# A finer account of time behind the order of two woven streams, and a later start for eight sets of blanks

## The chip, the cores and the metric

The kernel runs on one core of one Trainium2 chip. The time is device microseconds (us) of one launch, and the median over several launches counts. The core has five instruction queues that matter here: PE (TensorE, matmuls and transposes), ACT (ScalarE), DVE (VectorE), POOL (GpSimd) and SP (it only starts DMAs). Each works through its own instructions strictly in the order in which the program was written and waits for the others on semaphores. If the instruction at the head of a queue waits, everything behind it waits too.

## The reference

The model is a chain of sixteen residual steps on x of shape (8, 256, 128) in float32. Each one is `x = x + f(layernorm(x))`:

```
x = x + mamba(ln(x));             x = x + experts(ln(x))
x = x + linear_attention(ln(x));  x = x + experts(ln(x))
x = x + windowed_attention(ln(x)); x = x + channel_mix(ln(x))
x = x + delta_rule(ln(x));        x = x + channel_mix(ln(x))
x = x + state_space(ln(x));       x = x + low_rank_linear(ln(x))
x = x + mixed_attention(ln(x));   x = x + low_rank_linear(ln(x))
x = x + causal_attention_a(ln(x)); x = x + deep_network(ln(x))
x = x + causal_attention_b(ln(x)); x = x + deep_network(ln(x))
```

The two causal attentions have sixteen heads of eight elements. The state-space step is computed as a convolution with a filter that is worked out from its matrices A, B and C.

## The kernel before

**Two streams.** The batch of eight sequences is cut into four pairs, and a pair (512 tokens) goes through a layer at a time. Stream a takes pairs 0 and 2, stream b pairs 1 and 3. Each stream has four of the eight PSUM banks and its own working memory. Both run phase one (`mamba` to the second `channel_mix`) for their first pair and then for their second. They meet in `state_space`, which needs all four pairs, and then run phase two (`low_rank_linear` to the second `deep_network`) twice each. In the trace `stream_a` and `stream_b` are the buffers that hold a stream's normalized tokens and their transpose.

**How the order is made.** A layer is written as one Python generator for each engine (`tensor`, `scalar`, `vector`, `pool`, `sync`). It yields the signals that it waits for. The class `Weave` merges the lanes (one engine's program in one stream) into one order for each engine while the program is built. It keeps an account of time: each engine has a `free` time, each issued instruction adds a cost (`Lane.matmul`, `activation`, `vector` and others, L94 to L163), and its signals carry the time at which they would be raised. `Weave.run` (L222) always advances the lane with the smallest key:

```
key = (max(ready, e.free), lane.rank == BEHIND, ready, lane.rank)
```

`ready` is the accounted time of the signal that the lane waits for. So of the lanes of one engine the one whose signal came first goes first, and the costs decide which one that is. Nothing of this account exists at run time: only the order of the instructions in each queue is left of it.

**The lane behind.** `prepare` (L1765) computes the state-space filter on DVE and POOL (`product`, `power`, `back`, `ahead`, `filter`). It has the rank `BEHIND`, so it goes last among lanes whose time is equal. When its result is stored, `filter_loads` reloads the weights of the windowed attention (`held_l1a`), whose place in memory the filter's inputs had taken; the second pair's windowed attention waits for them.

**The blanks.** `small_heads` (L2179) is both causal attentions. Its heads are padded from 8 to 32 columns, and POOL writes the padding in five memsets (`wide_q`, `wide_k` twice, `wide_v` twice). Before them it waits for `s.rstd` (L2321), the signal for which the vector engine waits before it centres the tokens (`normalize`, L360 and after: four `tensor_scalar`, one for each 128 tokens, `stream_a<-x,moments,rstd` in the trace). PE's transposes of `wide_k` need the second blank, DVE's `placed` the fifth. Both also need the projected and copied q, k and v. `small_heads` is run eight times: two layers for four pairs.

## Time and profile before

| what | value |
|---|---|
| median of 3 runs | 3211.99 us (3210.1 to 3213.61) |
| the profiled execution | 3234.81 us |
| its span, first to last instruction | 3233.5 us |
| PE busy | 2634.1 us, 81% |
| DVE busy | 2104.3 us, 65% |
| ACT busy | 1429.0 us, 44% |
| POOL busy | 578.4 us, 18% |
| mean granted TensorE clock | 0.896 |

The span is one profiled execution. It lies 22.8 us above the median of the plain runs. Busy time of PE includes matmuls that run at the lower of the two clock levels, so it shrinks when the clock rises. An instruction is named by its source line: all matmuls are L108, transposes L111, activations L121, two-input vector operations L129, `tensor_scalar` L132, `scalar_tensor_tensor` L135, reductions L138, memsets L159. A float32 matmul is two instructions in the trace.

### The profile page before, as it was taken

The numbers are of one execution on the slowest core, as the hardware profiler recorded it, in microseconds if no ns is written. First come the engines' busy times: TensorE is split into PE (matmuls) and PEld (weight loads), VectorE is DVE, ScalarE is ACT, GpSimd is POOL, SyncE is SP. The second block draws the span as 40 slices with busy tenths as digits, with TensorE's granted clock in tenths as the row PEclk, the third lists the DMA queues.
The fourth block names the chain that finished last, engine by engine and source line by source line (L and its number), as shares of the span: only waits on it lengthen the run. The fifth ranks groups of instructions, "written<-read, shape, count | busy, mean of one in ns | idle before, by whom it ended". The sixth has DMA issues, their size and how long they took to land. (4 is left out here: it accounts for less than half of the span.)

```text
span 3233.5 us, 41136 instructions
## 1 busy us (share of the span) xinstructions
PE 2634.1 (81%) x15734; PEld 1707.1 (53%) x15734; DVE 2104.3 (65%) x4051; ACT 1429.0 (44%) x2577; POOL 578.4 (18%) x482
## 2 busy tenths in 40 slices
PE   5789897884878578989788689769878989778888
PEld 1267674452675224757454458459755455444554
DVE  6977887879988998888788675451264243552331
ACT  5533336774533553333477663340134335334342
POOL 2700001218760163000122064000010100000000
PEclk8999898996986699999889899569879999789899
DMA  3000001110000000000211200008200000000000
GB/s 146 0 1 1 1 1 33 40 34 4 1 1 1 0 1 32 1 1 1 76 40 40 66 1 2 0 1 273 86 1 2 1 1 1 7 1 1 1 2 7
DMA packets 51924, 73.18 MB, mean 23 GB/s; under 512 B 5776, under 2 KB 41360, under 8 KB 51088
## 3 DMA queue, kind: packets, MB, share of 16 engines
q1 hardware_dynamic: 51728, 70.56, 7.1%
q8 instruction: 124, 2.03, 0.3%
q14 instruction: 72, 0.59, 0.1%
HBM read 52.32 MB, written 1.44 MB: 17 GB/s over the span
## 5 line engine op out<-in xcount | busy, mean ns | idle before, releaser
L108 PEld LDWEIGHTS ps<-held_ffn,hidden 128*128 128x128 f32 x2304 | 299.4, 192 | 160.6 <-issue 110.4
L121 ACT ACTIVATE grown<-ps,bias_grown 128x512 f32<-128x512 f32 x288 | 197.9, 687 | 340.1 <-PE ps L108 333.6
L108 PE MATMUL ps<-held_ffn,hidden 128*128 128x128 f32 x2304 | 308.1, 277 | 24.4 <-DVE hidden L135 23.9
L129 POOL TENSOR_TENSOR qk<-conv,held_const 128x512 f32<-128x512 f32 x64 | 93.8, 1467 | 981.0 <-DVE conv L135 981.0
L135 DVE SCALAR_TENSOR_TENSOR conv<-conv_in,held_l1a,conv 128x512 f32<-128x512 f32 x288 | 228.5, 804 | 40.4 <-ACT conv L121 33.0
L129 POOL TENSOR_TENSOR long<-long,product 128x512 f32<-128x512 f32 x136 | 202.2, 1509 | 131.2 <-ACT product L121 123.6
L135 DVE SCALAR_TENSOR_TENSOR hidden<-ps,bias_kept,grown 128x512 f32<-128x512 f32 x288 | 211.6, 745 | 4.2
L132 DVE TENSOR_SCALAR grown<-grown,bias_fallen 128x512 f32<-128x512 f32 x288 | 140.1, 486 | 95.2 <-ACT grown L121 92.8
L159 POOL MEMSET wide_q<- 128x1536 f32 x8 | 11.0, 1378 | 978.9 <-ACT rstd L121 978.9
L129 POOL TENSOR_TENSOR part<-state,c_rows 128x512 f32<-128x512 f32 x128 | 163.1, 1302 | 97.3 <-issue 57.0
L138 DVE TENSOR_REDUCE wide_q<-ps 128x4 f32<-128x512 f32 (+1 forms) x128 | 114.4, 950 | 94.8 <-PE ps L108 94.7
L108 PE MATMUL ps<-part,held_const 128*128 128x512 f32 x256 | 151.2, 679 | 8.7 <-POOL part L129 5.3
L108 PE MATMUL ps<-stream_a,held_ffn 128*128 128x512 f32 x288 | 147.8, 597 | 2.3 <-ACT stream_a L121 2.3
L108 PE MATMUL ps<-stream_b,held_ffn 128*128 128x512 f32 x288 | 148.7, 601 | 0.7 <-ACT stream_b L121 0.7
L141 DVE TENSOR_TENSOR_SCAN state<-decay,ps 128x512 f32<-128x512 f32 x128 | 146.3, 1195 | 0.0
L108 PE MATMUL ps<-yn,nT 128*128 128x192 f32 (+1 forms) x640 | 113.8, 326 | 39.3 <-DVE yn L129 21.6
L121 ACT ACTIVATE probs<-ps 128x768 f32<-128x768 f32 x128 | 96.5, 808 | 97.4 <-PE ps L108 97.2
L144 DVE COPY outT<-ps 128x256 f32<-128x256 f32 x64 | 27.0, 421 | 156.7 <-PE ps L108 156.3
L108 PEld LDWEIGHTS ps<-yn,nT 128*128 128x128 f32 x640 | 100.1, 204 | 47.1 <-issue 36.6
L108 PE MATMUL ps<-u,ring 128*128 128x128 f32 (+3 forms) x1024 | 114.5, 275 | 1.2 <-DVE u L129 1.2
L108 PEld LDWEIGHTS ps<-u,ring 128*128 128x128 f32 x1024 | 114.4, 192 | 1.6 <-DVE u L129 1.6
L108 PE MATMUL ps<-a,held_l3f 128*128 128x512 f32 x256 | 111.6, 593 | 0.1
(442 smaller groups left out, 5717.1 us busy)
## 6 DMA issues: line engine op xcount, KB each, us to landing
ring<-lags SPq DMA_DIRECT2D x64, 512.0 KB, 4.5
turned<-conv SPq DMA_DIRECT2D x256, 64.0 KB, 2.0
held_ffn<-in_ffn SPq DMA_DIRECT2D x1, 4690.0 KB, 19.0
held_l1a<-in_l1a SPq DMA_DIRECT2D x2, 2120.0 KB, 15.9
held_l3f<-in_l3f SPq DMA_DIRECT2D x1, 2824.0 KB, 12.4
held_rows<-in_rows SPq DMA_DIRECT2D x1, 1044.5 KB, 8.3
out<-x SPq DMA_DIRECT2D x4, 256.0 KB, 2.6
held_const<-in_const SPq DMA_DIRECT2D x1, 785.0 KB, 4.6
```

Of the source, the lines that this page charges most:

```text
L108: return self.sent(self.real.matmul(out, lhsT, rhs, **kw), cost, 0.15)
L121: return self.sent(self.real.activation(out, a, func, **kw), cost)
L129: return self.vector(self.real.tensor_tensor(out, a, b, op), columns(out))
L132: return self.vector(self.real.tensor_scalar(out, a, p, q, *ops), columns(out))
L135: return self.vector(self.real.scalar_tensor_tensor(out, a, p, b, first, second), columns(out))
L138: return self.vector(self.real.tensor_reduce(out, a, axis, op, **kw), columns(a))
L141: return self.sent(self.real.tensor_tensor_scan(out, a, b, first, one, two), 0.16 + columns(out) / 460)
L144: return self.vector(self.real.tensor_copy(out, a), columns(out))
L159: return self.vector(self.real.memset(out, value), columns(out) // 2)
```

## The change

Four things are changed in the account, and one wait in the kernel. None of the arithmetic changes.

- PE's cost no longer is one number for each matmul. `Engine.blocks` is a grid of 4 by 4 array blocks with a time for each, so matmuls with a `tile_position` on different blocks may overlap and those on the same one queue. `Clock` keeps a level, fast or slow, by how much accounted matmul work fell into each past stretch, and doubles the cost of what starts in a slow one. Matmuls of four columns or fewer don't count as work.
- A vector operation without a PSUM operand, and every POOL operation that goes through `vector`, also waits for `Weave.shared`, one time that both engines share: they exclude each other in the account.
- Costs and tails of ACT, DVE and POOL instructions get other constants, the wait instruction costs nothing, and reciprocals, reductions and scans have formulas of their own.
- The first element of the key becomes `max(ready, e.free + 0.5)`, so a lane behind is taken only if no other lane of the same key time up to half a microsecond after `free` is ready.
- In `small_heads` POOL's blanks wait for `s.centred` at NT (all four centrings done) in place of `s.rstd`.

The diff:

```diff
@@ -59,11 +59,44 @@
     ACT.Sigmoid: 2}
 
 
+class Clock:
+
+
+    STRETCH, LITTLE, FULL = 3.41, 0.53, 0.9
+
+    def __init__(self):
+        self.fast = True
+        self.end = self.STRETCH
+        self.busy = 0.0
+        self.done = 0.0
+
+    def at(self, t):
+        while t >= self.end:
+            share = self.busy / self.STRETCH
+            self.fast = share >= self.LITTLE if self.fast else share >= self.FULL
+            self.end += self.STRETCH
+            self.busy = 0.0
+        return 1 if self.fast else 2
+
+    def worked(self, begin, end):
+        begin = max(begin, self.done)
+        if end <= begin:
+            return
+        self.done = end
+        if end > self.end:
+            self.busy += max(0.0, self.end - begin)
+            begin = max(begin, self.end)
+            self.at(self.end)
+        self.busy += end - begin
+
+
 class Engine:
 
     def __init__(self, name, real):
         self.name, self.real = name, real
         self.free = 0.0
+        self.blocks = np.zeros((4, 4))
+        self.clock = Clock()
         self.known = {}
         self.table = None
         self.spare = []
@@ -91,72 +124,87 @@
     def wait_ge(self, signal, n):
         return signal, n
 
-    def sent(self, ins, cost, latency=0.06):
+    def sent(self, ins, cost, tail):
         e = self.engine
         e.free += cost
-        return Sent(self, ins, e.free + latency)
+        return Sent(self, ins, e.free + tail)
+
+    def array(self, ins, cost, narrow=False, rows=slice(0, 4), cols=slice(0, 4)):
+        e = self.engine
+        begin = max(e.free, e.blocks[rows, cols].max())
+        slow = e.clock.at(begin)
+        end = begin + cost * slow
+        if not narrow:
+            e.clock.worked(begin, end)
+        e.blocks[rows, cols] = end
+        whole = e.blocks[rows, cols].size == e.blocks.size
+        e.free = end if whole else begin + 0.016
+        return Sent(self, ins, end + 0.15 + 0.05 * slow)
 
     def matmul(self, out, lhsT, rhs, **kw):
         n = columns(rhs)
-        slow = lhsT.dtype == F32
-        m = lhsT.shape[-1]
-        cost = max(n, 64) * (1.7 if slow else 0.43) / 1000
-        if "tile_position" in kw:
-            cost = cost / 3 + 0.015
-        else:
-            cost = max(cost, 0.225 if slow else 0.06)
-        return self.sent(self.real.matmul(out, lhsT, rhs, **kw), cost, 0.15)
+        ins = self.real.matmul(out, lhsT, rhs, **kw)
+        cost = max(n / 600, 0.223) if lhsT.dtype == F32 else max(n / 2400, 0.06)
+        if "tile_position" not in kw:
+            return self.array(ins, cost, n <= 4)
+        r, c = kw["tile_position"]
+        return self.array(ins, cost, n <= 4, slice(r // 32, (r + lhsT.shape[0] + 31) // 32),
+                          slice(c // 32, (c + lhsT.shape[-1] + 31) // 32))
 
     def transpose(self, out, a, ident):
-        return self.sent(self.real.transpose(out, a, ident), 0.112, 0.15)
+        return self.array(self.real.transpose(out, a, ident), 0.109)
 
     def activation(self, out, a, func, **kw):
-        cost = 0.19 + columns(out) / 960
         table = FUNCTION_SETS.get(func)
         if table is not None and table != self.engine.table:
             self.engine.table = table
-            cost += 1.3
+            self.engine.free += 1.3
             if table is EXP_AND_LN:
                 self.real.preload_act_table_set(EXP_AND_LN)
-        return self.sent(self.real.activation(out, a, func, **kw), cost)
-
-    def vector(self, ins, n):
-        if self.engine.name == "POOL":
-            return self.sent(ins, 0.12 + n / 400, 0.1)
-        return self.sent(ins, 0.16 + n / 960)
+        return self.sent(self.real.activation(out, a, func, **kw), 0.13 + columns(out) / 1150, 0.14)
+
+    def vector(self, ins, n, *of):
+
+        e, w = self.engine, self.weave
+        pool = e.name == "POOL"
+        cost = 0.1 + n / 460 if pool else 0.065 + n / 960
+        if pool or not any(a.space.name == "PSUM" for a in of):
+            e.free = max(e.free, w.shared)
+            w.shared = e.free + cost
+        return self.sent(ins, cost, 0.15 if pool else 0.13)
 
     def tensor_tensor(self, out, a, b, op):
-        return self.vector(self.real.tensor_tensor(out, a, b, op), columns(out))
+        return self.vector(self.real.tensor_tensor(out, a, b, op), columns(out), out, a, b)
 
     def tensor_scalar(self, out, a, p, q, *ops):
-        return self.vector(self.real.tensor_scalar(out, a, p, q, *ops), columns(out))
+        return self.vector(self.real.tensor_scalar(out, a, p, q, *ops), columns(out) // 2 + 40, out, a)
 
     def scalar_tensor_tensor(self, out, a, p, b, first, second):
-        return self.vector(self.real.scalar_tensor_tensor(out, a, p, b, first, second), columns(out))
+        return self.vector(self.real.scalar_tensor_tensor(out, a, p, b, first, second), columns(out) + 60, out, a, b)
 
     def tensor_reduce(self, out, a, axis, op, **kw):
-        return self.vector(self.real.tensor_reduce(out, a, axis, op, **kw), columns(a))
+        return self.sent(self.real.tensor_reduce(out, a, axis, op, **kw), 0.065 + columns(a) / 960, 0.13)
 
     def tensor_tensor_scan(self, out, a, b, first, one, two):
-        return self.sent(self.real.tensor_tensor_scan(out, a, b, first, one, two), 0.16 + columns(out) / 460)
+        return self.sent(self.real.tensor_tensor_scan(out, a, b, first, one, two), 0.04 + columns(out) / 480, 0.13)
 
     def tensor_copy(self, out, a):
-        return self.vector(self.real.tensor_copy(out, a), columns(out))
+        return self.vector(self.real.tensor_copy(out, a), columns(out), out, a)
 
     def reciprocal(self, out, a):
-        return self.vector(self.real.reciprocal(out, a), columns(out))
+        return self.sent(self.real.reciprocal(out, a), 0.065 + columns(out) / 150, 0.13)
 
     def max(self, out, a):
-        return self.vector(self.real.max(out, a), columns(a))
+        return self.sent(self.real.max(out, a), 0.065 + columns(a) / 960, 0.13)
 
     def bn_stats(self, out, a):
-        return self.vector(self.real.bn_stats(out, a), columns(a))
+        return self.sent(self.real.bn_stats(out, a), 0.065 + columns(a) / 960, 0.13)
 
     def bn_aggr(self, out, a):
-        return self.vector(self.real.bn_aggr(out, a), 24)
+        return self.sent(self.real.bn_aggr(out, a), 0.08, 0.12)
 
     def memset(self, out, value):
-        return self.vector(self.real.memset(out, value), columns(out) // 2)
+        return self.vector(self.real.memset(out, value), columns(out) // 2, out)
 
     def dma_start(self, out, a):
         self.engine.free += 0.1
@@ -177,6 +225,7 @@
         self.engines = {name: Engine(name, real) for name, real in (
             ("PE", nc.tensor), ("ACT", nc.scalar), ("DVE", nc.vector), ("POOL", nc.gpsimd), ("SP", nc.sync))}
         self.made = 0
+        self.shared = 0.0
 
     def raised(self, lane, signal, ins, by, at):
         engine = lane.engine
@@ -213,7 +262,6 @@
             if e.known.get(signal.sem.num, 0) < signal.base + n:
                 e.known[signal.sem.num] = signal.base + n
                 e.real.wait_ge(signal.sem, signal.base + n)
-                e.free += 0.02
         try:
             lane.asked = next(lane.program)
         except StopIteration:
@@ -229,7 +277,7 @@
                     ready = 0.0 if lane.asked is None else lane.asked[0].when(lane.asked[1])
                     if ready is None:
                         continue
-                    key = (max(ready, e.free), lane.rank == BEHIND, ready, lane.rank)
+                    key = (max(ready, e.free + 0.5), lane.rank == BEHIND, ready, lane.rank)
                     if best is None or key < best[0]:
                         best = key, lane
             if best is None:
@@ -2318,7 +2366,7 @@
 
     def pool(po):
         yield from n_.pool(po)
-        yield po.wait_ge(s.rstd, 1)
+        yield po.wait_ge(s.centred, NT)
         po.memset(b.wide_q[:, :, :, D:], 0.0).then_inc(s.blank)
         po.memset(c.wide_k[:, :, :, D:D + 1], 1.0).then_inc(s.blank)
         po.memset(c.wide_k[:, :, :, D + 1:], 0.0).then_inc(s.blank)
```

## Rows read from the trace of the kernel before

**Rows 1.** The page, part 1: busy time, share of the span, instructions.
```profile
PE 2634.1 (81%) x15734; PEld 1707.1 (53%) x15734; DVE 2104.3 (65%) x4051; ACT 1429.0 (44%) x2577; POOL 578.4 (18%) x482
```

**Rows 2.** Busy time by stretch: window, engines' busy us, PEclk, DMA share, GB/s.
```profile
730.00:1090.00 360.00, 252.62 (x1395) 190.52 (x1396) 331.83 (x513) 155.39 (x255) 183.91 (x148) 0.76 0.01 1
...
1850.00:2185.00 335.00, 268.17 (x1444) 203.35 (x1445) 199.53 (x407) 150.87 (x244) 89.78 (x68) 0.79 0.00 1
...
2330.00:2760.00 430.00, 370.90 (x2731) 219.52 (x2732) 173.64 (x397) 176.04 (x284) 20.88 (x24) 0.93 0.00 1
2760.00:3180.00 420.00, 344.47 (x2675) 209.67 (x2673) 163.57 (x359) 152.96 (x255) 21.00 (x24) 0.91 0.01 2
```

**Rows 3.** Timeline of DVE at the end: stream a behind stream b's network.
```profile
3174.08 0.26 DVE L147 RECIPROCAL inverse<-ps 128x16 f32<-128x16 f32 x1 [13.91 <-PE ps L111]
```

**Rows 4.** Last projection before the state-space step, by stream.
```profile
L108 PE MATMUL ps<-held_l2a,stream_a x16: 379/380/634, 2136.3 to 2151.3; 128*128 128x256 f32 x16
...
L108 PE MATMUL ps<-held_l2a,stream_b x16: 379/559/634, 2167.3 to 2181.3; 128*128 128x256 f32 x16
```

**Rows 5.** The chain that ended last, in order of time: start us, us, what.
```profile
2377.83 3.00 DVE stream_b L132 x3
...
2583.08 4.45 DVE stream_a L132 x3
...
2986.75 3.13 DVE stream_b L132 x4
```

**Rows 6.** Timeline of DVE, 2370 to 2400 us: start us, us, what, instructions.
```profile
2370.07 1.12 DVE L132 TENSOR_SCALAR stream_b<-x,moments,rstd 128x128 f32<-128x128 f32 x4 [1.27 <-ACT rstd L121]
...
2390.20 1.74 DVE L129 TENSOR_TENSOR qkv<-qkv,held_rows 128x1536 f32<-128x1536 f32 x1
...
2397.47 1.76 DVE L129 TENSOR_TENSOR qkv<-qkv,held_rows 128x1536 f32<-128x1536 f32 x1 [2.59 <-ACT qkv L121]
```

**Rows 7.** Timeline of POOL, same stretch: the first blank and the last.
```profile
2377.85 1.38 POOL L159 MEMSET wide_q<- 128x1536 f32 x1 [391.28 <-ACT rstd L121]
...
2390.07 1.58 POOL L159 MEMSET wide_v<- 128x64 f32 x2
```

**Rows 8.** Groups of instructions by form: busy us, mean ns, idle before.
```profile
L132 DVE TENSOR_SCALAR grown<-grown,bias_fallen 128x512 f32<-128x512 f32 x288 | 140.1, 486 | 95.2 <-ACT grown L121 92.8
...
L121 ACT ACTIVATE probs<-ps 128x768 f32<-128x768 f32 x128 | 96.5, 808 | 97.4 <-PE ps L108 97.2
...
L129 DVE TENSOR_TENSOR product<-power 128x1024 f32<-128x1024 f32 x24 | 53.9, 2246 | 0.3
```

**Rows 9.** Timeline of PE in windowed attention, 600 to 612 us.
```profile
604.52 0.76 PE L108 MATMUL ps<-probs,v 128*64 128x192 f32 x8
...
605.12 0.71 PE L108 MATMUL ps<-probs,ones 128*64 128x192 f32 x8
...
605.76 1.16 PE L108 MATMUL ps<-held_const,square 128*128 128x128 f32 x8
```

**Rows 10.** Timeline of PE in small heads, 2879 to 2891 us.
```profile
2881.18 0.94 PE L108 MATMUL ps<-kT,qT 32*128 32x128 f32 x16 [1.13 <-DVE wide_q L138]
...
2882.05 0.61 PE L108 MATMUL ps<-after,ident 128*128 128x256 bf16 x4
...
2882.59 0.94 PE L108 MATMUL ps<-qT,kT 32*128 32x256 f32 x16
```

**Rows 11.** Mixed attention's casts of each stream: first and last start.
```profile
L144 DVE CAST x<-stream_a x2: 421/424/426, 2338.5 to 2786.9; 128x512 f16<-128x512 f32 x2
...
L144 DVE CAST x<-stream_b x2: 428/428/428, 2333.7 to 2751.3; 128x512 f16<-128x512 f32 x2
```

**Rows 12.** Reload and first use of held_l1a in the second pass.
```profile
L108 PEld LDWEIGHTS ps<-stream_a,held_l1a x30: 186/190/338, 1559.4 to 1682.3; 128*128 128x128 f32 x30
...
L164 SPq DMA_DIRECT2D held_l1a<-in_l1a x1: 344/344/344, 1277.2 to 1277.2; - x1
```

**Rows 13.** Busy time in the stretch from the second mamba to that use.
```profile
1087.00:1620.00 533.00, 439.11 (x2024) 261.72 (x2022) 448.58 (x896) 232.62 (x392) 94.40 (x76) 0.93 0.05 17
```

## The prediction

> **What bounds the kernel now.** The page's busy times come first [rows 1]. PE works 81% of the span, DVE 65%, and no engine is full, so the time is PE's work plus the stretches in which PE waits. The account that the change rewrites can touch only the second part: 3233.5 less 2634.1 is 599 us of idle PE in the whole span. The windows by stretch say where it lies [rows 2]. In the first delta rule (730 to 1090 us) DVE is busy 331.8 of 360 us and PE 252.6; the same layers in the second pass (1850 to 2185) take 335 us with DVE busy only 199.5. In phase two (2330 to 2760 and 2760 to 3180) PE is busy 370.9 of 430 and 344.5 of 420 us, which leaves 135 us idle, and DVE, ACT and POOL are mostly idle. These are stretches of two dependency chains that take turns on PE. There a better order can win.
>
> Two places show what a bad order costs and what this change leaves as it is. At 3174 us stream a's reciprocal has waited 13.91 us for PE [rows 3], since its transposes stand in PE's queue behind the dense matmuls of stream b's network. The key still prefers the lane with the oldest signal, and a network's matmuls wait on signals that are long past, so a finer cost doesn't move that wait. And before the state-space step stream a starts its last input projection at 2151.3 us and stream b at 2181.3 us [rows 4]: the streams arrive 30 us apart, and the second one decides.
>
> **The blanks.** The chain that ended last runs through six of the eight centrings in front of small heads. Three of them stand in [rows 5]; the six last 3.00, 3.07, 4.45, 4.44, 3.14 and 3.13 us, together 21.2 us. The same four instructions take 1.12 us in front of the low-rank layer, where POOL is idle [rows 6]. In small heads POOL's first memset starts at 2377.85 us, 0.02 us after the centring in [rows 5], on the same signal, and each centring instruction waits its turn among the memsets. Behind the change the memsets start when the centring is done. Removed from the chain: 21.2 less 6 x 1.12, so 14.5 us; the two others lose some 2 us each beside the chain. The other stream's work is as near in some of these places, so I count 12 of the 14.5. The bounds are 0 (all of it hidden behind the other stream) and 15.
>
> What the moved memsets may delay: a set lasts 1.38 + 1.58 + 1.58 = 4.5 us [rows 7]. It would end 1.1 + 4.5 = 5.6 us after the centring begins. The stream's first DVE work on q, k and v comes 12.4 us after it (2377.8 to 2390.2) in the one case and 10.3 us (2387.15 to 2397.47) in the other [rows 6], so projections and copies cover the blanks with 4 us to spare; without that cover each set would cost up to 4.5 us, 36 us for eight. The sets can still catch a `tensor_scalar` of the other stream, for at most one memset, 1.6 us, at a time. That stays inside the 2.5 us that I left off the 14.5.
>
> **The costs, against the rows.** An order improves only where the account comes nearer to the chip. For `grown` (512 columns, `tensor_scalar` from SBUF) the old cost is 0.693 us, the new one 0.373 and a tail of 0.13; the row says 0.486 [rows 8]. For the 768-column `probs` on ACT old is 0.99, new 0.80; busy time over count is 96.5 / 128 = 0.754 us [rows 8]. In windowed attention a group of mixing matmuls on two column blocks starts 0.60 to 0.64 us after the one before [rows 9]; old 0.42, new 0.54. In the stretches of [rows 2] the granted clock means 0.76 and 0.79, so part of them ran at 1.2 instead of 2.4 GHz, which the old account never shows and the new one at least tries to. Against it: in small heads the sixteen score matmuls on four row blocks hold PE from 2881.18 to 2882.05, 0.87 us [rows 10]. Old says 0.99, new 0.65, so here the old one is nearer. And `product<-power` takes 2.246 us [rows 8], while old says 1.23 and new 1.13: both let the filter in as a thing half its size. The account gets nearer in four of six kinds.
>
> The lock is the other new part. At 2390.20 DVE adds a bias to q, k and v, two inputs from SBUF, and takes 1.74 us while POOL's memset of 1.58 us begins at 2390.07; the same addition with POOL idle takes 1.76 us [rows 6, 7]. A memset doesn't hold up that instruction, but the new account says that it does. By the row the moved blanks cost such additions nothing; by the account each set would put the addition off by up to 1.6 us, 13 us for eight sets, a delay that exists only on paper and sets ready times wrongly. The Trainium skill (SBUF — State Buffer, the section on the two separate sides) has the same split: a vector operation with two SBUF inputs is blocked only against a GpSimd operation that reads SBUF. By that rule, the new lock is too strict at the memsets, and the trace agrees.
>
> **The lane behind.** The first delta rule takes 25 us more than the second (360 against 335), and the filter's work lies in it: DVE is busy 331.8 us there and 199.5 in the second, so the filter takes 132 us of DVE, 53.9 of them in 24 of its products [rows 2, 8]. Under the old key a product of 2.2 us could start when another lane was due 0.05 us later. The half microsecond forbids that. Bounds: 0 (the gaps are long anyway) and 25 (the first pass becomes as short as the second). I take 5, since the products last 2.2 us and still run over any gap of 0.5.
>
> **The rest of the order.** The trace can't show an order that hasn't run; it bounds what order alone is worth. Stream a needs 448.4 us from one mixed attention to the next, stream b 417.6, for the same layers [rows 11]: 31 us by who goes first. I take a third of this as a gain, 10 us, because four of six costs come nearer, and both ends, 30 faster and 30 slower.
>
> **The sum**, on the profiled execution: 3234.8 - 12 - 5 - 10 = 3207.8 us. The profiled execution is 22.8 us above the median of the plain runs, so against 3212.0 the forecast is 3185 us. The terms' ends give 3212 - 15 - 25 - 30 = 3142 and 3212 + 30 = 3242.
>
> **The rivals.**
> - *Only the blanks act*: the two streams have one order forced by their chains nearly everywhere, and 12 us go: 3200. For it: most PE queues alternate strictly. Against it: costs that move by 30 to 45% [rows 8, 9].
> - *Nothing shows*: the other stream's chain lies right under all six centrings and takes their place: 3212. Against it: they are on the chain that ended last.
> - *The streams draw together*: the 30 us between the arrivals before the state-space step vanish, half of the gap is won there, and the other terms stand near their ends (12, 15 and 20): 3212 - 62 = 3150.
> - *The streams draw apart*, the other side: a less suited order of PE and DVE in the delta rule, where the lock misjudges POOL, lets the first stream run ahead, and the second one arrives later. Each microsecond of further distance at the join [rows 4] costs one. From 18.4 us on it outweighs the blanks and the 0.2% that can be told from no change; a distance twice as long costs 30: 3212 - 12 + 30 = 3230.
> - *The filter comes late*: the half microsecond keeps it out of so many gaps that the reload of `held_l1a`, now started at 1277.2 us and used at 1559.4 [rows 12], holds up both streams. From 1087 us to a little behind that use DVE is idle 533 - 448.6 = 84 us [rows 13]. If all of the filter's 132 us move there, 48 us are late, while the first delta rule gains its 25: 3212 - 12 - 25 + 48 = 3223. Below 84 us moved nothing is late, and only near 130 does it end slower.
>
> **How the numbers follow.** Forecast 0.42 (3165 to 3204), only the blanks 0.18, nothing 0.07, drawing together 0.13, drawing apart 0.17, late filter 0.03. A measurement of this kernel can tell about 0.2%, 6.4 us, from no change. Faster than 3205.6: 0.42 + 0.13 + 0.11 of the blanks' case, 0.66. Within: 0.07 + 0.07, 0.14. Slower than 3218.4: 0.20. The range goes from 3135, a little under the rival at 3150, to 3236, just above the one at 3230; the late filter and half of what draws apart are left out.
>
> **What the changed profile would show.** The eight centrings at 1.1 us, with the first memset behind their end; none of the small heads' centrings above 1.7 us. First input of the second windowed attention not waiting on the reload. Filter products spread further out than 1087 us, and the first delta rule under 360 us. Less than 599 us of idle PE. The prediction is wrong if the idle time is as before but has moved, above all to 2100 to 2185 us, or if the reload stands in the chain.

## The result, and the profile after

The changed kernel takes 3084.94 us in the median (3082.87 to 3089.42), against 3212.8 us before: a ratio of 0.9597, 95% interval 0.9575 to 0.9619. That is 128 us or 4.0% faster. The forecast was 3185 us with a range from 3135 to 3236. The sign was right; the size was not, and the time lies outside the range.

The page of the changed kernel, its first lines:

```profile
span 3081.5 us, 41110 instructions
## 1 busy us (share of the span) xinstructions
PE 2574.1 (84%) x15734; PEld 1687.9 (55%) x15734; DVE 2116.9 (69%) x4051; ACT 1415.8 (46%) x2561; POOL 553.4 (18%) x482
```

PE, DVE and POOL have as many instructions as before, in another order. ACT has 16 fewer (2577 and 2561): its order also decides how often it must load another table of functions, and it loads 91 times instead of 107, at 1.28 us each. The gain doesn't hang on that: all_but_lock below loads 110 times, and its profiled execution has nearly the same span (3081.0 us). PE's idle time fell from 599 us [rows 1] to 3081.5 - 2574.1 = 507 us. PE's busy time fell by 60 us with the same 15734 matmuls; the mean granted clock rose from 0.896 to 0.906. A part of this belongs to the one execution shown before. The run `blanks_alone` below has the order of before and a clock of 0.904:

```profile
PE 2609.0 (82%) x15734; PEld 1697.0 (53%) x15734; DVE 2090.7 (65%) x4051; ACT 1429.2 (45%) x2577; POOL 575.7 (18%) x482
```

Its span is 3200.5 us, so PE is idle for 591.5 us. Against it the changed kernel has 84 us less of idle PE and 35 us less of busy PE. About half of the latter lies in phase two, where the same 5657 instructions of PE take 754.8 us instead of 772.5 at a granted clock of 0.95 instead of 0.92.

The costliest groups of DVE after the change (busy us, mean ns | idle before them and what ended it) show the same work at nearly the same length (`conv` is 5% longer), but with less waiting in front of it:

```profile
L183 DVE SCALAR_TENSOR_TENSOR conv<-conv_in,held_l1a,conv 128x512 f32<-128x512 f32 x288 | 238.7, 848 | 16.0 <-ACT conv L164 12.9
...
L180 DVE TENSOR_SCALAR grown<-grown,bias_fallen 128x512 f32<-128x512 f32 x288 | 138.5, 482 | 53.5 <-ACT grown L164 47.7
L186 DVE TENSOR_REDUCE wide_q<-ps 128x4 f32<-128x512 f32 (+1 forms) x128 | 113.5, 952 | 48.5 <-PE ps L146 48.5
```

In the kernel before `grown` waited 95.2 us [rows 8], and the two others:

```profile
L135 DVE SCALAR_TENSOR_TENSOR conv<-conv_in,held_l1a,conv 128x512 f32<-128x512 f32 x288 | 228.5, 804 | 40.4 <-ACT conv L121 33.0
...
L138 DVE TENSOR_REDUCE wide_q<-ps 128x4 f32<-128x512 f32 (+1 forms) x128 | 114.4, 950 | 94.8 <-PE ps L108 94.7
```

DVE isn't the busiest engine, so these waits are a sign of a better order and not its price. The gain isn't in one place. The table sets the changed kernel beside `blanks_alone`, whose queues hold the instructions of the kernel before in its order, with the blanks' wait moved as in the change. So the differences are those of the order alone. Its profiled execution (3201.8 us) lies near the median of its runs, where the one shown before lies 22.8 us above. The marks are the first windowed projection of stream a, the last transposes of `oT`, the last `x<-x,y` of each pass, and the last filter matmul `ps<-u,ring`.

| stretch, us | order before, blanks moved | after | difference |
|---|---|---|---|
| start to first windowed attention | 485.8 | 478.9 | -6.9 |
| windowed attention, first pass | 237.2 | 222.9 | -14.3 |
| channel mixes and delta rule, first pass | 365.4 | 355.5 | -9.9 |
| mamba to second windowed attention | 460.4 | 454.6 | -5.8 |
| windowed attention, second pass | 258.1 | 227.3 | -30.8 |
| channel mixes and delta rule, second pass | 340.9 | 314.1 | -26.8 |
| to the end of the state-space matmuls | 138.4 | 141.5 | +3.1 |
| phase two | 914.3 | 886.7 | -27.6 |

The sum is -119.0 us, and the blanks come on top of it. Set against the length of the stretch, the largest differences stand in the second pass: 12% of its windowed attention and 8% of its channel mixes and delta rule. The two stretches with mamba and the experts, where PE was busy for 83 and 86% of the time, gave little, and so did phase two for its length (3%).

The centrings before small heads, and POOL's blanks, in the timelines of the changed kernel (start us, us, what):

```profile
2264.28 1.12 DVE L180 TENSOR_SCALAR stream_b<-x,moments,rstd 128x128 f32<-128x128 f32 x4 [0.68 <-ACT rstd L164]
2267.79 2.15 DVE L180 TENSOR_SCALAR stream_a<-x,moments,rstd 128x128 f32<-128x128 f32 x4 [0.60 <-ACT rstd L164]
```

```profile
2265.52 1.38 POOL L207 MEMSET wide_q<- 128x1536 f32 x1 [339.21 <-DVE stream_b L180]
```

Stream b's four instructions last 1.12 us instead of 3.00 [rows 5], and the first memset begins behind them, at 2265.52 us. Stream a's centring at 2267.79 meets stream b's memsets, which run to 2269.8, and one of its instructions is held up: 2.15 us. That is the collision that the prediction priced at one memset at most; here it cost 1.0 us. The other seven of these centrings take 1.11 to 1.12 us.

The reload of the windowed attention's weights and its use, and the arrivals before the state-space step (instruction count: min/median/max ns, first and last start us):

```profile
L146 PE MATMUL ps<-stream_a,held_l1a x48: 592/592/1222, 1511.9 to 1702.0; 128*128 128x512 f32 x48
L146 PE MATMUL ps<-stream_b,held_l1a x48: 592/592/1222, 1517.9 to 1710.1; 128*128 128x512 f32 x48
...
L212 SPq DMA_DIRECT2D held_l1a<-in_l1a x1: 345/345/345, 1419.1 to 1419.1; - x1
```

```profile
L146 PE MATMUL ps<-held_l2a,stream_a x16: 379/634/635, 2041.0 to 2060.1; 128*128 128x256 f32 x16
L146 PE MATMUL ps<-held_l2a,stream_b x16: 379/440/634, 2063.5 to 2077.2; 128*128 128x256 f32 x16
```

The filter is done later than before (the reload starts at 1419.1 us, not 1277.2 [rows 12]), but the reload starts 93 us ahead of its use. The two streams enter the second windowed attention within 6 us of each other. At the join they are 17 us apart, where it was 30 [rows 4].

### The profile page after: what moved, and what is told of

It is laid out like the page before. It is cut to its first block and busy times, and to the rows that moved or that the text cites. A ratio compares the mean times of both kernels' runs of the same rounds, so it can differ in the third digit from the quotient of the medians.

```text
span 3081.5 us, 41110 instructions
## 1 busy us (share of the span) xinstructions
PE 2574.1 (84%) x15734; PEld 1687.9 (55%) x15734; DVE 2116.9 (69%) x4051; ACT 1415.8 (46%) x2561; POOL 553.4 (18%) x482
## 5 line engine op out<-in xcount | busy, mean ns | idle before, releaser
L183 DVE SCALAR_TENSOR_TENSOR conv<-conv_in,held_l1a,conv 128x512 f32<-128x512 f32 x288 | 238.7, 848 | 16.0 <-ACT conv L164 12.9
L177 POOL TENSOR_TENSOR long<-long,product 128x512 f32<-128x512 f32 x136 | 191.9, 1450 | 156.4 <-ACT product L164 154.8
L180 DVE TENSOR_SCALAR grown<-grown,bias_fallen 128x512 f32<-128x512 f32 x288 | 138.5, 482 | 53.5 <-ACT grown L164 47.7
L146 PE MATMUL ps<-part,held_const 128*128 128x512 f32 x256 | 157.4, 721 | 7.4 <-POOL part L177 5.6
L186 DVE TENSOR_REDUCE wide_q<-ps 128x4 f32<-128x512 f32 (+1 forms) x128 | 113.5, 952 | 48.5 <-PE ps L146 48.5
```

Of the source, the lines that this page charges most:

```text
L146: ins = self.real.matmul(out, lhsT, rhs, **kw)
L177: return self.vector(self.real.tensor_tensor(out, a, b, op), columns(out), out, a, b)
L180: return self.vector(self.real.tensor_scalar(out, a, p, q, *ops), columns(out) // 2 + 40, out, a)
L183: return self.vector(self.real.scalar_tensor_tensor(out, a, p, b, first, second), columns(out) + 60, out, a, b)
L186: return self.sent(self.real.tensor_reduce(out, a, axis, op, **kw), 0.065 + columns(a) / 960, 0.13)
```

## Experiments

Each run is timed against the kernel before on the same chip. Times of before differed from chip to chip and run to run (3202 to 3236 us), so the ratios with their 95% intervals are what to compare; the changed kernel's 0.9597 comes from a measurement of its own. The profiled execution of a run is one of its executions. First the parts alone, then the controls, then the costs taken apart, then the changed kernel less one part, then the late filter, and last two attempts to better the account. None leaves out any of the computation. Most edits are shown by their main lines only.

### The parts alone

**blanks_alone**: only the moved wait. All four engines' queues hold the same instructions in the same order as before.

```diff
-        yield po.wait_ge(s.rstd, 1)
+        yield po.wait_ge(s.centred, NT)
```

> The kernel before with only the moved blanks; the account stays, so apart from small heads' start the order is made by the same rules. Theory 'the order did it': the eight centrings shrink from 3.0 to 4.5 us to about 1.1, and 8 to 15 us go: 3198 to 3204, ratio 0.995 to 0.998. Rival 'the blanks are the lever': the shorter lock of the port changes how the streams meet in phase two, and most of the 48 us that phase two lost go: about 3165, ratio 0.985.

Measured: 3201.34 us, ratio 0.9944 (0.9926 to 0.9962), 18 us (12 to 24). The eight centrings in front of small heads last 1.11 to 1.12 us. So the blanks give 18 us with the order untouched. The interval covers the 14.5 us that I had read off the chain, and the 12 that I took lie at its lower end. The moved memsets do catch a centring of the other stream, and for more than one memset: stream a's at 2958.27 us, in front of another layer, takes 3.26 us, 2.1 more than undisturbed (in the profile before such a one took 2.11). The blanks don't carry the result.

**key_alone**: only the half microsecond.

```diff
-                    key = (max(ready, e.free), lane.rank == BEHIND, ready, lane.rank)
+                    key = (max(ready, e.free + 0.5), lane.rank == BEHIND, ready, lane.rank)
```

> The kernel before with only the half microsecond in the key. Theory 'better costs did it': the filter is spread out, the first delta rule loses up to 10 us, the rest stays: ratio 0.995 to 1.0. Rival 'the lane behind was the disturbance': the filter's 2.2 us products stop cutting into both streams and at least 40 us go (the first pass and the second mamba): ratio 0.987 or less.

Measured: 3196.67 us, ratio 0.9926 (0.991 to 0.9942), 24 us, between the two expectations. The trace tells why. The last experts of the first stretch are done, and then PE stands still. The busy times of 1533 to 1584 us (PE, PEld, DVE, ACT, POOL), and pieces of the chain there:

```profile
1533.00:1584.00 51.00, 0.00 (x0) 0.00 (x0) 38.52 (x39) 0.57 (x1) 0.00 (x0) 0.50 0.33 123
```

```profile
1573.82 2.31 DMA lags<-filter
...
1576.15 8.14 DMA held_l1a<-in_l1a
...
1584.34 2.09 PE ps L108 x2
```

The filter was kept out of so many gaps that what is left of it runs alone, while both streams wait for the reload: 51 us with no matmul at all. This is the prediction's rival of the late filter, in full. It is outweighed by what the key gives elsewhere: the first delta rule with its mixes takes 341.6 us here (365.4 in blanks_alone, 370.0 in the profile before). The second takes 307.9 us where it took 340.9. Behind the stall the streams enter the second windowed attention 2 us apart; whether that shortened what follows isn't shown.

**costs_alone**: the new costs and tails of ACT, DVE and POOL, free waits; PE's old account, no lock, the old key, the old blanks. The core of it:

```diff
-        cost = 0.19 + columns(out) / 960
+        cost = 0.13 + columns(out) / 1150
...
-            return self.sent(ins, 0.12 + n / 400, 0.1)
-        return self.sent(ins, 0.16 + n / 960)
+        cost = 0.1 + n / 460 if pool else 0.065 + n / 960
+        return self.sent(ins, cost, 0.15 if pool else 0.13)
...
-                e.free += 0.02
```

> The kernel before with only the new costs and tails of ACT, DVE and POOL (and waits at no cost); PE's old account, no lock, the old key, the old blanks. Theory 'the vector and scalar costs carry it': more than half of the 128 us go, ratio 0.98 or less, in all stages. Rival 'PE's account carries it': ratio 0.99 to 1.0 here.

Measured: 3163.42 us, ratio 0.9814 (0.9783 to 0.9845), 60 us. It's the largest part, but at the median a little under half of the whole.

**pe_alone**: only PE's account, that is `Clock`, `Engine.blocks`, `Lane.array` and the new constants of matmuls and transposes.

```diff
-        return self.sent(self.real.matmul(out, lhsT, rhs, **kw), cost, 0.15)
...
+            return self.array(ins, cost, n <= 4)
```

> The kernel before with only PE's blocks and two-level clock (with the longer tail of matmuls that belongs to them). Theory 'PE's account carries it': more than half of the 128 us go, ratio 0.98 or less, most in the delta rule and windowed attention, where the clock is low or matmuls sit on blocks. Rival 'the vector and scalar costs carry it': ratio 0.99 to 1.0.

Measured: 3197.9 us, ratio 0.9939 (0.9917 to 0.9961), 20 us. Both theories of one carrier are wrong in their pure form: the four parts multiply to 0.9944 x 0.9926 x 0.9814 x 0.9939 = 0.963, close to the 0.9597 of all together.

### Controls: is it the nearness to the chip?

**scaled_up**: every cost in the old account 5% larger, so that the proportions are as wrong as before.

```diff
-        e.free += cost
+        e.free += 1.05 * cost
```

> Control: the kernel before with every cost of PE, ACT, DVE and POOL multiplied by 1.05 in the account; the relative costs are as wrong as before. Theory 'a truer account orders better': no systematic gain, the time moves only by the scatter of a disturbed order, ratio 0.99 to 1.01. Rival 'the old order was an unlucky one and any disturbance betters it': ratio 0.985 or less.

Measured: 3219.32 us, ratio 1.0021 (1.0004 to 1.0037). This control is weaker than it was meant to be, since it hardly changes the order. Compared place by place, by operation and names, PE's queue differs from before's in 286 of 15734 places and DVE's in 99 of 4051; for costs_alone it is 6455 and 2329. So it doesn't show that the order of before was no unlucky one, nor how much a large change of order moves the time by chance.

**costs_away**: the costs of costs_alone mirrored at the old ones. For most DVE operations:

```diff
-        return self.sent(ins, 0.16 + n / 960)
+        old = 0.16 + n / 960
+        return self.sent(ins, 2 * old - (0.065 + n / 960 if new is None else new))
```

> The kernel before with the costs, tails and wait costs of ACT, DVE and POOL moved by the same steps as in the changed kernel, but the other way (each is twice the old value less the new one, tails 0 and 0.05 us). Theory 'nearer to the chip is what orders better': the time rises by 1 to 2.5%, ratio 1.01 to 1.025, the mirror of 0.981. Rival 'any change of relative costs betters an unlucky order': ratio below 0.995.

Measured: 3266.86 us, ratio 1.0168 (1.0137 to 1.0199). Toward the chip -1.9%, away from it +1.7%. This order differs much from before's (4303 places of PE's queue, 2261 of DVE's), and it is the only one of the large reorderings tried here that is slower than before. But it's no clean mirror. Its filter comes late, as in key_alone: the reload starts at 1598.9 us, and PE stands still in front of it (window, busy us of PE, PEld, DVE, ACT, POOL):

```profile
1571.60:1607.10 35.50, 0.00 (x0) 0.00 (x1) 23.27 (x22) 0.60 (x1) 0.00 (x0) 0.50 0.46 177
```

Before had no gap of PE above 2 us in front of its first projection there. So this one gap is 35.5 of the 53.7 us that were lost, and about 18 us are left for everything else (an estimate from these two numbers). The two delta rules with their mixes are even shorter than in the profile before (349.0 and 325.9 us after 370.0 and 342.9), and phase two is as long (933.1 after 934.6), where costs_alone takes 888.6 us.

DVE's idle time in front of `grown` and `conv` goes the way of the time. In costs_away (last part of the line: idle us before the group):

```profile
L136 DVE SCALAR_TENSOR_TENSOR conv<-conv_in,held_l1a,conv 128x512 f32<-128x512 f32 x288 | 239.1, 842 | 76.3 <-ACT conv L121 67.6 <-PE ps L108 3.5
...
L133 DVE TENSOR_SCALAR grown<-grown,bias_fallen 128x512 f32<-128x512 f32 x288 | 140.4, 488 | 109.7 <-ACT grown L121 109.1
```

and in costs_alone:

```profile
L169 DVE SCALAR_TENSOR_TENSOR conv<-conv_in,held_l1a,conv 128x512 f32<-128x512 f32 x288 | 237.7, 832 | 39.8 <-PE ps L141 22.0 <-ACT conv L153 14.4
...
L166 DVE TENSOR_SCALAR grown<-grown,bias_fallen 128x512 f32<-128x512 f32 x288 | 140.9, 490 | 79.4 <-ACT grown L153 73.9
```

From away over before to costs_alone and the changed kernel `grown` waits 109.7, 95.2, 79.4 and 53.5 us, `conv` 76.3, 40.4, 39.8 and 16.0. The busy time of `grown` stays between 138.5 and 140.9 us and that of `conv` between 228.5 and 239.1. What shrinks is the idle time of DVE at the head of its queue. Not every group follows: `wide_q` waits 87.6, 94.8, 37.3 and 48.5 us, and between before and costs_alone `conv` doesn't change. Which wrong cost put which instruction too early isn't shown.

### The costs taken apart

**tails_alone**: old costs, results of ACT and DVE seen 0.14 us after them instead of 0.06, of POOL 0.15 instead of 0.10.

```diff
-    def sent(self, ins, cost, latency=0.06):
+    def sent(self, ins, cost, latency=0.14):
```

> The kernel before with only longer tails: a result of ACT or DVE is seen 0.14 us behind the end of its cost in place of 0.06, POOL's 0.15 in place of 0.10; costs as before. Theory 'the costs by kind carry it (tensor_scalar, reciprocals, ACT)': ratio 0.995 to 1.005. Rival 'the tails carry it, since a chain then shows its true latency': ratio 0.985 or less, most of what the new costs gave (0.981).

Measured: 3188.63 us, ratio 0.9915 (0.99 to 0.9931), between the two expectations.

**costs_old_tails**: costs_alone with the tails of before.

```diff
+        tail = tail if e.name == "PE" else 0.1 if e.name == "POOL" else 0.06
         return Sent(self, ins, e.free + tail)
```

> The new costs of ACT, DVE and POOL (and free waits) without their tails: results are seen 0.06 and 0.10 us after the cost's end, as before. PE, key, lock and blanks as before. Theory 'costs by kind and tails each carry half' (the tails alone gave 0.9915, both together 0.9814): ratio 0.988 to 0.992. Rival 'cost and tail only work as a sum': the shorter costs with short tails make all latencies too short, ratio 1.0 or more. Third: costs carry it nearly alone, 0.985 or less.

Measured: 3151.76 us, ratio 0.981 (0.9783 to 0.9836), the same as with the tails. The third case of the expectation holds: the costs by kind carry it. Longer tails better the old costs by 0.85% but add nothing to the new ones, so these two parts don't add.

**vector_costs_alone** and **act_costs_alone**: the new costs of DVE and POOL with free waits, and the new cost of ACT, each with old tails. The edit of the second:

```diff
-        cost = 0.19 + columns(out) / 960
+        cost = 0.13 + columns(out) / 1150
```

> The kernel before with the new costs of DVE and POOL only (waits free, old tails, old ACT costs). Theory 'DVE's costs carry it' (tensor_scalar 0.69 to 0.37, reciprocals and short instructions halved, most handed from chain to chain): ratio 0.981 to 0.986. Rival 'ACT's cost carries it': 0.993 or more.

> The kernel before with only ACT's new cost (0.13 + n/1150 for 0.19 + n/960). Theory 'DVE's costs carry it': ratio 0.995 to 1.0. Rival 'ACT's cost carries it': 0.988 or less.

Measured: 3178.99 us, ratio 0.9875 (0.9833 to 0.9916), and 3202.27 us, ratio 0.9945 (0.9922 to 0.9969). The first is a little short of its expectation, the second a little better than its. Both matter, the vector side twice as much; multiplied 0.982, which agrees with 0.981.

### The changed kernel less one part

```diff
 all_but_lock
-        if pool or not any(a.space.name == "PSUM" for a in of):
-            e.free = max(e.free, w.shared)
-            w.shared = e.free + cost
 all_but_clock
-        slow = e.clock.at(begin)
+        slow = 1
 all_but_pe
-            return self.array(ins, cost, n <= 4)
+        return self.sent(self.real.matmul(out, lhsT, rhs, **kw), cost, 0.15)
 all_but_key
-                    key = (max(ready, e.free + 0.5), lane.rank == BEHIND, ready, lane.rank)
+                    key = (max(ready, e.free), lane.rank == BEHIND, ready, lane.rank)
 all_but_blanks
-        yield po.wait_ge(s.centred, NT)
+        yield po.wait_ge(s.rstd, 1)
```

> The changed kernel without the shared time of DVE and POOL. Theory 'the four other parts add up' (0.9944, 0.9926, 0.9814 and 0.9939 multiply to 0.963): ratio 0.960 to 0.966 against the kernel before. Rival 'the lock is a part of its own': 0.970 or more. If the lock is too strict at memsets and does harm: below 0.957.

> The changed kernel with PE's account always at the fast level (blocks kept). Theory 'the clock is the part of PE's account that counts', since the stretches with a mean granted clock of 0.6 to 0.8 are modelled at half the true matmul time: it loses most of what the whole PE account gives there (0.974 against 0.960), ratio 0.970 or more. Rival 'the blocks and the per-instruction times count': 0.958 to 0.963.

> The changed kernel with PE's old account. Theory 'parts add up': it loses what PE's account gave alone, 0.96 / 0.994: ratio 0.966. Rival 'PE's account only helps where the other costs are already right': it loses 1.5% or more, ratio 0.975 or more. If PE's account does nothing there: 0.960.

> The changed kernel without the half microsecond. Theory 'parts add up': ratio 0.960 / 0.993 = 0.967, with the first delta rule 10 to 30 us longer. Rival 'the lock and truer costs already keep the filter out': ratio 0.958 to 0.962. The filter should be done near 1100 to 1280 us instead of 1393.

> The changed kernel with the blanks waiting for rstd again. Theory 'parts add up': it loses what they gave alone, ratio 0.960 / 0.9944 = 0.965. Rival 'a better order hides the centring behind the other stream': 0.961 or less, with the centrings at 3 us or more again but off the chain.

| kernel | median us | ratio to before | 95% interval |
|---|---|---|---|
| changed kernel | 3084.94 | 0.9597 | 0.9575 to 0.9619 |
| all_but_lock | 3098.47 | 0.9633 | 0.9602 to 0.9664 |
| all_but_clock | 3104.34 | 0.9659 | 0.9633 to 0.9684 |
| all_but_key | 3105.58 | 0.9665 | 0.964 to 0.9691 |
| all_but_blanks | 3114.03 | 0.9669 | 0.9626 to 0.9713 |
| all_but_pe | 3126.16 | 0.9738 | 0.9715 to 0.976 |

The blanks are worth 0.7% here and 0.6% alone, the key 0.7% in both: these add up. A better order doesn't hide the centring. The whole PE account is worth 1.4% here against 0.6% alone, so it is worth more beside the other costs, as the rival of all_but_pe had it, though the ratio stays a little under the rival's 0.975. Without the clock 0.6% is lost, between the two expectations, about half of that. The lock's 0.4% can't be told from nothing, since the intervals overlap; what all_but_lock gives (0.9633) is what the four other parts multiply to.

### The late filter

**key_until_1150**: key_alone, but the half microsecond ends when the account stands at 1150 us, so that the filter can be finished in the experts.

```diff
-                    key = (max(ready, e.free), lane.rank == BEHIND, ready, lane.rank)
+                    key = (max(ready, e.free + (0.5 if e.free < 1150 else 0.0)), lane.rank == BEHIND, ready, lane.rank)
```

> The kernel before with the half microsecond only while the account stands under 1150 us; behind that the lane behind is taken as before, so the filter can be done before the second windowed attention. Theory 'the late filter ate half of what the key gave' (a stall of 40 to 50 us near 1533 to 1584 us): the reload starts before 1450 us, and the ratio is 0.980 to 0.985 against 0.9926. Rival 'the stall was free, since it brought the streams together for the second delta rule': ratio 0.990 to 0.995 again.

Measured: 3171.6 us, ratio 0.9854 (0.9813 to 0.9896), against 0.9926 of key_alone. The reload started only at 1552.0 us (the expectation said before 1450), yet the first projection came at 1560.1 instead of 1584.3. PE still stands still in front of it, from 1542.4 us on, 17.7 us instead of 51. So with 34 us less of the stall the key gives 42 us by the medians and 47 by the ratio, where it gave 24. What it gives without any stall wasn't measured.

### Two attempts at a still nearer account

**lock_by_rows**: the changed kernel with a lock after [rows 6, 7]. `tensor_scalar` and copies in SBUF (they pass `wide`) and all POOL operations exclude each other; operations with two SBUF inputs only exclude POOL operations that read SBUF. Unlike the expectation says, DVE's own memsets are left free.

```diff
-        if pool or not any(a.space.name == "PSUM" for a in of):
-            e.free = max(e.free, w.shared)
-            w.shared = e.free + cost
+        from_sbuf = not any(a.space.name == "PSUM" for a in of)
+        if pool:
+            e.free = max(e.free, w.port, w.reads if len(of) > 1 else 0.0)
+            w.shared = e.free + cost
+            if len(of) > 1:
+                w.pool_reads = e.free + cost
+        elif from_sbuf and wide:
+            e.free = max(e.free, w.shared)
+            w.port = e.free + cost
+        elif from_sbuf and len(of) > 2:
+            e.free = max(e.free, w.pool_reads)
+            w.reads = e.free + cost
```

> The changed kernel with a lock as the rows show it: tensor_scalar, copies and memsets of DVE in SBUF and every POOL operation exclude each other, additions and the like with two SBUF inputs only against POOL operations that read SBUF, reductions and the rest never. Theory 'nearer is better': ratio 0.953 to 0.959 against the kernel before, under the changed kernel's 0.960. Rival 'what is left is scatter': 0.959 to 0.965.

Measured: 3114.92 us, ratio 0.9676 (0.9645 to 0.9706). It's worse than either expectation. The first pass is as in the changed kernel (its last `x<-x,y` at 1058.6 us against 1057.3), and then the streams drift. Its second windowed attention, and its arrivals at the join:

```profile
L146 PE MATMUL ps<-stream_a,held_l1a x48: 592/592/1061, 1500.5 to 1686.6; 128*128 128x512 f32 x48
L146 PE MATMUL ps<-stream_b,held_l1a x48: 592/592/807, 1546.2 to 1738.8; 128*128 128x512 f32 x48
```

```profile
L146 PE MATMUL ps<-held_l2a,stream_b x16: 379/434/634, 2096.6 to 2110.3; 128*128 128x256 f32 x16
...
L146 PE MATMUL ps<-held_l2a,stream_a x8: 634/634/774, 2055.5 to 2058.7; 128*128 128x256 f32 x8
```

The streams enter the second windowed attention 46 us apart, not 6, and reach the join 52 us apart, not 17. Stream a comes to the join when it did in the changed kernel (2058.7 against 2060.1 us); stream b comes 33 us later, and the state-space matmuls start 33 us later (2113.6 against 2080.5). That is the whole difference of the two spans, 3113.8 less 3081.5. It's the prediction's rival of streams that draw apart, seen at last, though in a variant.

**filter_priced**: the changed kernel with the filter's first 32 products counted at 2.09 us instead of 1.13.

```diff
+        if self.rank == BEHIND and self.engine.name == "DVE" and (n == 1024 and self.engine.products < 32):
+            self.engine.products += 1
+            n = 2 * n - 100
```

> The changed kernel with the filter's first 32 products on DVE counted as 1948 columns (2.09 us) instead of 1024 (1.13 us). Theory 'nearer is better': first delta rule 5 to 15 us shorter, ratio 0.955 to 0.959. Rival 'it is put into gaps anyway': 0.959 to 0.962. Third: the account sees the filter as dearer, the reload comes later than its present 1419 us and may stall: 0.963 or more.

Measured: 3120.51 us, ratio 0.9719 (0.9672 to 0.9767), its runs from 3104 to 3138 us. The first pass is indeed shorter: its last `x<-x,y` comes at 1040.4 us, 17 us earlier than in the changed kernel, as the first theory says. It is given back: the join's arrivals are 38 us apart, and the state-space matmuls start at 2092.7 us, 12 us later. A local improvement was real and was lost at the barrier. The ratio is the one of the third expectation, but not for its reason: the reload doesn't come later than in the changed kernel (1406.1 us, 1419.1 there) and stalls nothing. The profiled execution is also the fastest of the four, so the trace explains only a part of the loss.

## Why the prediction was right in sign and wrong in size

- **The blanks** (12 us, bounds 0 and 15): right mechanism, the size somewhat low. They gave 18 us with the order untouched, 0.56% (0.38 to 0.74%, or 12 to 24 us), so the median lies above my upper bound, and the interval begins at about my term. Whether the 2.5 us that I took off and the two centrings that I left out were right can't be told within it. Two of my details were wrong: a set can hold up the other stream for more than one memset (2.1 us in blanks_alone), and of the small heads' centrings one took 2.15 us, where I had said that none would be above 1.7. That additions with two SBUF inputs go unhindered beside memsets was right, and the cover behind the centring held.
- **The lane behind** (5 us, bounds 0 and 25): mis-sized. Alone it gave 24 us in spite of a stall of 51 us, and 42 to 47 us with the stall cut to 17.7. The bound of 25 came from comparing the first and the second delta rule, and supposed that the key acts only there.
- **The rest of the order** (10 us, bounds -30 and 30): this is the step that failed, and by its size, not its way. Costs and PE's account gave 60 and 20 us alone, and of the 128 us about 86 are left for this term when the blanks' 18 and the key's 24 are taken off (an estimate from the single runs). I had bounded what another order is worth by the difference between the two streams under one order, 31 us [rows 11]. But both of those go through the same merge, so their difference says nothing about what all of them lose to it. I had also looked for the gain in the delta rules and in phase two, the windows of [rows 2]; by the table the new order gave 27.6 us in phase two, beside the blanks, and 91 us in phase one, 45 of them in the two windowed attentions, which I hadn't looked at.
- **What an order can touch**: I had said that the account touches only the 599 us in which PE is idle. Most of the gain is there, 84 us of the 119 between blanks_alone and the changed kernel, but 35 us came out of PE's busy time.
- **The rivals**: the streams did come closer at the join, 17 us against 30, as the rival at 3150 us had it, but that is 13 of 128 us. The late filter doesn't happen in the changed kernel (93 us of slack) and does in key_alone. Drawing apart doesn't happen in it and does in lock_by_rows, at one microsecond a microsecond, as priced.
- **The doubts about the account**: that its lock is too strict and that it counts filter products at half their length are both true on the rows. Neither costs anything that could be shown, since mending either made the kernel slower.
- **The signs that I had named**: idle PE fell under 599 us, the filter ran on beyond 1087 us (to 1393), the second windowed attention didn't wait for the reload, and the first delta rule with its mixes took 355.5 us.

Shown is which part of the change gave what. What stays open is whether these orders are better because the account is nearer to the chip. For it: each of the new parts alone gave 0.6 to 1.9%, and the one account that was moved away gave an order 1.7% slower. Against it: two thirds of that loss are one late reload, the control with equally wrong costs left the order nearly as it was, and every single alteration of the changed kernel cost something, 0.4 to 1.4%, also the two that brought the account nearer to the rows. Part of that is the worth of the removed piece (blanks and key repeat what they gave alone), part can be that this order also falls well at the join. A large reordering that is neither nearer nor farther, random cost errors of the old size for example, would tell; it wasn't tried. Which of DVE's formulas (`tensor_scalar`, reciprocals, free waits) carries the vector side's 1.2% wasn't tried.

## What to carry to other kernels

Where a program's order comes from an account of costs, check the account against the profile kind by kind. The old one had `grown` 43% and `probs` 31% too long, and new costs for ACT, DVE and POOL alone were worth 2% of time here, with the same matmuls and vector operations. Don't bound what a new order can win by the difference between two parts that the same order made: 31 us by that, about 86 measured. The bottleneck's idle time (here 599 us) is the wider and safer measure, though even it isn't all, since 35 us came out of PE's busy time. Test such an account with several orders, and look for a stall in each: a control can fail by hardly changing the order, or by running into a wait of its own. And follow a local gain to the next point where the streams meet: what one stream wins before a barrier is lost if the other comes later.

## What the runs showed of the hardware

A memset on POOL holds up a `tensor_scalar` between SBUF tensors, but not an addition of two SBUF inputs: the four instructions of a centring in front of small heads took 2.76 to 4.50 us beside memsets in the kernel before and 1.11 to 1.12 in blanks_alone, while the 1536-column addition took 1.74 beside a memset and 1.76 alone [rows 5 to 7]. Two executions of programs with the same order (before and blanks_alone) were 13 us apart at the start of the state-space step (2184.7 and 2171.9 us), before the only wait in which they differ: that much of a profile's difference can be the execution alone.
